# Cross-attention's inputs loaded and prepared during self-attention, and a round's turns ahead of the pair's output projection

## What is computed

```python
x = x + attn(layernorm(x), wq, wk, wv, wo)                 # 16 heads of 64
x = x + xattn(layernorm(x), ctx, mask, Wq, bq, Wk, bk, Wv, bv, Wo, bo)   # 16 heads of 16
x = x + ffn(layernorm(x), ...)                             # 8 experts, one per token
```

## Time and profile before

| | |
|---|---|
| median of 3 runs | 1658.84 us (1657.04 to 1662.4) |
| profiled execution, in all | 1658.88 us |
| its span | 1657.1 us |
| busy in the span: TensorE | 1446.5 us (87%) |
| VectorE | 962.8 us (58%) |
| ScalarE | 760.2 us (46%) |
| Pool | 563.7 us (34%) |

### The profile page before, as it was taken

How to read it: one execution, slowest core, us unless ns; L and a number is a source line. 1 busy time by engine, 2 the same in 40 slices (tenths; PEclk the granted TensorE clock), 3 DMA queues, 4 the chain that set the end, 5 groups by cost and what they waited for, 6 DMA issues and landing times. The chain is left out here.

```text
span 1657.1 us, 39281 instructions
## 1 busy us (share of the span) xinstructions
PE 1446.5 (87%) x12244; PEld 1250.0 (75%) x12244; DVE 962.8 (58%) x2371; ACT 760.2 (46%) x1830; POOL 563.7 (34%) x692
## 2 busy tenths in 40 slices
PE   4789899999999998479999999999986119999997
PEld 3688878888887877368888888888866118888886
DVE  5547475656566665157777777767653215555553
ACT  4547464655555565035655555555651002222221
POOL 5244353525252617512222222222202443333332
PEclk9899999999999999679999999999995559999999
DMA  5703030303021221387676666767621413555551
GB/s 180 208 2 81 1 79 2 77 13 66 17 62 34 45 44 37 78 216 193 179 198 180 189 186 184 199 176 200 172 73 53 143 57 126 188 184 189 180 182 51
DMA packets 159950, 195.71 MB, mean 118 GB/s; under 512 B 83724, under 2 KB 128307, under 8 KB 159636
## 3 DMA queue, kind: packets, MB, share of 16 engines
q1 hardware_dynamic: 154356, 186.09, 40.6%
q0 software_dynamic: 3968, 6.59, 1.2%
q10 hardware_dynamic: 1568, 2.30, 0.5%
HBM read 138.63 MB, written 58.05 MB: 119 GB/s over the span
## 5 line engine op out<-in xcount | busy, mean ns | idle before, releaser
L1209 DVE TENSOR_REDUCE row_max<-psb_s 100x1 f32<-100x361 f32 x512 | 263.4, 531 | 140.1 <-PE psb_s L1352 134.2
L1101 ACT ACTIVATE probs<-psb_t 121x400 f32<-121x400 f32 (+1 forms) x384 | 190.5, 508 | 115.2 <-PE psb_t L1362 112.5
L1352 PE MATMUL psb_s<-k,q 97*100 97x362 f32 x512 | 185.3, 364 | 15.2 <-DVE row_max L1209 9.4
L437 POOL TENSOR_TENSOR diag<-neg_ident,row_max 100x400 fp32r<-100x400 f32 x128 | 112.2, 898 | 183.0 <-DVE row_max L529 158.2
L1362 PE MATMUL psb_t<-q,k 98*121 98x200 f32 (+1 forms) x768 | 147.5, 274 | 1.9 <-ACT probs L1101 1.7
L2032 PE MATMUL psd_h<-h_in,w_sb 128*128 128x256 f32 x640 | 144.2, 384 | 1.4 <-ACT h_in L1898 1.4
L2040 PE MATMUL psd_y<-w_sb,hid 128*128 128x256 f32 x640 | 144.5, 379 | 0.0
L2032 PEld LDWEIGHTS psd_h<-h_in,w_sb 128*128 128x128 f32 x640 | 123.5, 193 | 19.0 <-issue 1.8
L2040 PEld LDWEIGHTS psd_y<-w_sb,hid 128*128 128x128 f32 x640 | 120.1, 190 | 15.5
L1362 PEld LDWEIGHTS psb_t<-q,k 98*121 98x121 f32 (+1 forms) x768 | 125.4, 184 | 6.1 <-ACT probs L1101 2.7
L1352 PEld LDWEIGHTS psb_s<-k,q 97*100 97x100 f32 x512 | 85.7, 168 | 41.5 <-DVE row_max L1209 27.2
(11 more groups left out here) (226 smaller groups left out, 3604.6 us busy)
## 6 DMA issues: line engine op xcount, KB each, us to landing
w_sb<-in_w SPq DMA_DIRECT2D x40, 1024.0 KB, 7.6
packed_keys<-k_st SPq DMA_DIRECT2D x32, 724.0 KB, 3.5
k<-packed_keys SPq DMA_DIRECT2D x64, 362.0 KB
v_rows<-v_tok SPq DMA_DIRECT2D x32, 400.0 KB
v_ext<-v_rows SPq DMA_DIRECT2D x32, 400.0 KB
q<-packed_queries SPq DMA_DIRECT2D x64, 200.0 KB
k<-packed_keys SPq DMA_DIRECT2D x64, 181.0 KB
c_t<-in_contextT SPq DMA_DIRECT2D x32, 361.0 KB, 4.6
```

What stands on the lines that cost most here:

```text
L437: pool.tensor_tensor(diag[:, g % 2], c.neg_ident[0:S, 0:S].unsqueeze(1).to_broadcast([S, GH, S]), row_max[:, g // 2 % 2, g % 2].unsqueeze( ...
L1101: act.activation(probs[0:KT[kt], u % 2, kt], ps_t[i % 2][0:KT[kt], 0:4 * S], ACT.Exp, scale=HD2 ** -0.5).then_inc(probs_ready, 1)
L1209: dve.reduce_max(row_max[:, p, h:h + 1], ps_s[h % 2][0:S, 0:S2], AX_X).then_inc(max_ready, 1)
L1352: pe.matmul(ps_s[h % 2][0:S, 0:S2E], q2[0:97, p, u, g, S * a:S * (a + 1)], k2[0:97, p, u, g], start=True, stop=True).then_inc(scores_ready, 1)
```

## The change

Two edits, and what they need.

1. Cross-attention's buffers for wk, wv, wq, the biases, the masks and the first context now lie in `c.stage`, the same memory as w_stage, which outlives self-attention. o_part moves to its end. SP takes quad 0 out of its loop and issues the loads of `cross_inputs` behind quad 0's value transfers. Pool clears the mask buffers behind the weight split and computes the masks ahead of the last quad. wo and bo are loaded at the start of cross-attention behind the second context. Rows q2[96] and k2[97] get their ones by two loads from HBM instead of two memsets on Pool. At the start of cross-attention Pool begins with split_context(0), and all engines put the first keys ahead of the first turned x. normalize(0) on VectorE stands behind keys(0, 0, 0). The clearing of v_ext comes behind split_context(1).
2. In self-attention TensorE's turns of round r-2 stand ahead of the pair's projection.

Some semaphores that nobody waits for are shared between blocks.

```diff
 def self_attention (SP):
+            def cross_inputs():
+                sp.wait_ge(vo_lo_ready, 2)
+                for dst, src in ((c.wk_st, cross["wk"]), (c.wv_st, cross["wv"]), (c.wq_sb, cross["wq"])):
+                    sp.dma_start(dst, src.rearrange("(k p) n -> p k n", p=128)).then_inc(c.cross["w2_loaded"], 16)
+                for dst, src in ((c.bq_sb, cross["bq"]), (c.bk_sb, cross["bk"]), (c.bv_sb, cross["bv"])):
+                    sp.dma_start(dst, src).then_inc(c.cross["w2_loaded"], 16)
+                sp.dma_start(c.first_context, cross["ctxT"][0].rearrange("(k p) s -> p k s", p=128)
+                             ).then_inc(c.cross["ctx_loaded"], 16)
+                sp.dma_start(cross["qd"]..., c.empty...).then_inc(c.cross["q_cleared"], 16)
+                sp.dma_start(cross["ones"], c.ones_f[:]).then_inc(c.cross["ones_stored"], 16)
+                sp.wait_ge(c.cross["mask_cleared"], 2)
+                for kt in range(3):
+                    sp.dma_start(c.mask_t[0:KT[kt], kt, :], cross["maskT"][KT0[kt]:KT0[kt] + KT[kt], :]
+                                 ).then_inc(c.cross["mask_t_loaded"], 16)
+                sp.dma_start(c.mask_b[:, 0:S2], cross["mask"]).then_inc(c.cross["mask_b_loaded"], 16)
+            values_through(0)
+            cross_inputs()
+            with sp.Fori(1, QUADS) as q:
+                values_through(q)
+            sp.wait_ge(c.cross["bias_ready"], 1)
+            sp.dma_start(cross["kb"], c.bias_b.bitcast(F32)).then_inc(c.cross["bias_stored"], 16)
+            sp.wait_ge(c.cross["bias_stored"], 16)
+            sp.wait_ge(c.cross["ones_stored"], 16)
+            sp.wait_ge(c.cross["q_cleared"], 16)
 (Pool):
             split_weights(1)
+            pool.wait_ge(vo_lo_ready, 2)
+            pool.memset(c.mask_t, 0).then_inc(c.cross["mask_cleared"], 1)
+            pool.memset(c.mask_b, 1).then_inc(c.cross["mask_cleared"], 1)
...
             with pool.Fori(1, QUADS - 1) as q:
                 quad(q, False)
+            cross_masks()
             quad(QUADS - 1, True)
 (TensorE), in iteration r, behind the diagonals:
+                    for g in in_round(r - 2):
+                        ...  (the turns of L702)
                     for g in in_round(r - 3):
                         if last_round_of_pair(r - 3):
                             ...  (the projection)
-                    for g in in_round(r - 2):
-                        ...  (the turns of L702)
 def cross_attention (SP):
             context(1, 1)
+            sp.dma_start(wo_sb, wo.rearrange("(k p) n -> p k n", p=128)).then_inc(wo_loaded, 16)
+            sp.dma_start(bo_sb, bo...to_broadcast([S, D])).then_inc(wo_loaded, 16)
+            sp.dma_start(q2[96:97]..., ones(16 * 2 * S)).then_inc(ones_placed, 16)
+            sp.dma_start(k2[97:98]..., ones(16 * S2E)).then_inc(ones_placed, 16)
 (Pool):
+            split_context(0, 0)
             inverse_root(0)
-            split_context(0, 0)
+            split_context(1, 1)
             inverse_root(1)
-            split_context(1, 1)
+            pool.memset(v_ext[:, :, :, :, HD2:32], 0.0).then_inc(pad_ready, 1)
 (VectorE):
-            dve.wait_ge(w_lo_ready, 2)
             norm_stats(0)
+            low_bits(0, wk_hi, wk_lo, wk_st)
+            low_bits(1, wv_hi, wv_lo, wv_st)
+            keys(0, 0, 0)
             normalize(0)
             norm_stats(1)
             normalize(1)
             norm_stats(2)
-            keys(0, 0, 0)
 (TensorE):
-            pe.wait_ge(w_loaded, 16 * 8)
-            pe.wait_ge(w_hi_ready, 2)
-            pe.wait_ge(w_lo_ready, 2)
-            pe.wait_ge(pad_ready, 5)
+            pe.wait_ge(w_loaded, 16 * 6)
+            pe.wait_ge(w_lo_ready, 1)
+            pe.wait_ge(pad_ready, 2)
+            keys(-2, 0, 0)
             turn_x(-3, 1)
-            keys(-2, 0, 0)
...
+            pe.wait_ge(w_lo_ready, 2)
             values(-1, 1, 0)
+            pe.wait_ge(ones_placed, 32)
```

More of the change, by code:

```diff
@@ L109, in at_batch, with stage_for_cross_attention, take, weight @@
     return tensor[:, bass.ds(b, 1), cols].rearrange("p b d -> p (b d)")
-def self_attention(nc, c, x, wqkT, wvT, woT, v_dram, xs):
+def stage_for_cross_attention(c, ctx, nc):
+    at = [0]
+    def take(words):
+        at[0] += words
+        return c.stage[:, at[0] - words:at[0]]
+    def weight():
+        return take(KD * D).rearrange("p (k n) -> p k n", k=KD)
+    c.wk_st, c.wv_st, c.wq_sb = weight(), weight(), weight()
+    c.bq_sb, c.bk_sb, c.bv_sb = take(KD), take(KD), take(KD)
+    c.mask_t, c.key_dead, c.key_live = (take(3 * B)[0:KT[0]].rearrange("p (k b) -> p k b", k=3) for _ in range(3))
+    c.mask_t = c.mask_t.bitcast(I32)
+    c.mask_b = take(S2E)[0:B].bitcast(I32)
+    c.bias_b = take(S2E)[0:B].bitcast(F32R)
+    c.first_context = take(KD * S2).rearrange("p (k s) -> p k s", k=KD)
+    at[0] = 2 * KD * O1 - 4 * (S // GB) * NT
+    c.wo_sb = weight()
+    c.bo_sb = take(D)[0:S]
+    for name in ("w2_loaded", "mask_cleared", "mask_t_loaded", "mask_b_loaded", "key_mask_ready", "bias_ready",
+                 "bias_stored", "ctx_loaded", "q_cleared", "ones_stored"):
+        c.cross[name] = ctx.enter_context(nc.semaphore(name + "_x"))
+def self_attention(nc, c, x, wqkT, wvT, woT, v_dram, xs, cross):
     with ExitStack() as ctx:
@@ L679, in quad @@
                                   skip_group_check=True).then_inc(shifted_ready, 1)
+                    for g in in_round(r - 2):
+                        pe.wait_ge(o_ready, q * GQ + (g + 1))
+                        if g == 0:
+                            reach(pe, x1_ready, q * QUAD)
+                        if g >= 2:
+                            pe.wait_ge(ot_copied_act, q * 2 * GQ + 2 * (g - g % 2))
+                        for w in range(2):
+                            ins = pe.transpose(ps_ot[:, 2 * S * (g % 2) + S * w:2 * S * (g % 2) + S * (w + 1)],
+                                               o_norm[:, g % 2, 128 * w:128 * (w + 1)], c.ident[0:S, 0:S])
+                        ins.then_inc(ot_ready, 1)
                     for g in in_round(r - 3):
@@ L969, in step @@
                     place(b + 2, p)
-            sp.wait_ge(q_cleared, 16)
             place(0, 0)
```

169 lines of the change are left out of this document (73 added, 96 removed).

## The result

The changed kernel takes 1637.33 us (median of four executions, 1635.16 to 1639.22); the kernel before, executed beside it, 1657.94 (1653.13 to 1662.4). The ratio is 0.9872, with an interval of 0.9844 to 0.9900: 20.6 us faster, where 16.7 were worked out. The profiled spans are 1634.5 and 1657.1 us, 22.6 us apart.

What follows compares the result with a forecast made beforehand. TensorE was taken to bound what follows its hollow at the change to cross-attention. An earlier start (14.4 us) and the turns (2.3) sum to 16.7 us, giving a 1640.4 us span and 1642.1 us time, range 1636 to 1649.

Steps and rivals of the forecast that it cites:

- The bound: TensorE's hollow at the change to cross-attention, a 21.3 us wait for xn; earlier first scores should carry to the end.
- Cost 0 for what moved: Loads, small memsets and mask operations moved into self-attention fit in idle time; SP's 10.2 us of issuing fits into 55.7.
- Step 1 and 2: From T, SP's first issue of cross-attention: Pool's split to T+2.7, plus 0.69 us for VectorE's wk subtraction, first keys T+3.4.
- The barrier: Start of cross-attention: TensorE and ScalarE starting behind the barrier cost 0, with up to 3 us left in the range.
- Step 3 and 4: First keys' matmuls and low part free VectorE at T+6.8; normalize(0), beside Pool's second context, ends at T+7.9.
- Step 5: Turn of xn, its copy and the first queries in cross-attention: queries' low part ready at T+12.3.
- Step 6: Stores and packed loads before the first scores, untouched: 11.5 us, first scores at T+23.8 against T+38.2, gain 14.4 us.
- The turns, 8 x 0.29: Self-attention, round 6 of each quad: turns inside TensorE's 1.68 us wait for o_lo gain 2.3 us, bounds 0 and 4.1.
- The kinder clock: Rival at cross-attention's start: clock stays 2.4 GHz or engines do not hold; gain 18 to 22, about 1638.5 us, chance 0.2.
- A new wait: Rival: late engines, Pool's second context ahead of normalize(0), or packed loads meeting other transfers; 1648 us, chance 0.2.
- The slower rival: Self-attention: turns ahead of the projection wait for a late o_norm; at 3.9 us late about 1662 us, chance 0.03.
- The change doesn't do what it says: Rival: first scores wait for something that stays, so cross-attention's start moves by less than 4 us; 1655 us, chance 0.04.

Runs made afterwards that it cites:

- the loads alone: The changed kernel with the pair's projection put back ahead of TensorE's turns in self-attention; 1644.84 us, ratio 0.9899.
- the clearing late: The changed kernel with SP's clearing of routed_rows issued behind the moved cross-attention loads instead of ahead of quad 0's value stores; 1630.25 us, ratio 0.9818.
- wv later: The changed kernel with VectorE's wv subtraction behind keys(0,0,0), normalize(0) and norm_stats(1); 1640.84 us in one execution.
- the turns alone: The kernel before with only TensorE's turns of round r-2 moved ahead of the pair's projection; 1654.78 us, ratio 0.9972.

## Why the prediction was right, point by point

- **The bound.** Right. The hollow was the place, and the shift of the first scores was kept: 532.36 and 532.19 us from there to routing.
- **Cost 0 for what moved.** Right. SP's moved loads stand after quad 0's value loads, in order of time in the changed kernel:

```profile
71.33 2.22 SPq L338 DMA_DIRECT2D v_ext<-v_rows  x2
73.59 2.57 SPq L345 DMA_DIRECT2D stage<-in_wk2T  x1
...
84.53 0.32 SPq L357 DMA_DIRECT2D stage<-in_mask  x1
```

  They end at 84.85 us, 11.3 us of issuing where 10.2 were put, long ahead of the store of quad 1. The sum left out the store of ones, 3.28 us, and read the end of the old list at 683.66, where the load of the mask behind it ends at 684.03. No wait of TensorE or VectorE is new there.
- **Step 1 and 2, first keys at T+3.4.** T+3.08. c_lo took 1.91 us beside the subtraction of wk against 1.58 alone: the two do hold each other off, but Pool lost 0.33 and not the whole 0.69, since wk's subtraction had begun 0.31 us ahead of c_lo. The Trainium skill says that Pool contends with VectorE instructions that have two SBUF inputs (GPSIMD Engine Reference, 1. Specifications). The trace agrees: both subtractions have two, and they grew from 1.58 to 1.91 (c_lo) and from 0.66 to 2.07 us (wv_lo).
- **The barrier.** Up to 3 us were left in the range for a late start of ScalarE and TensorE. ScalarE starts at T+0.02, and TensorE 0.14 us behind the end of c_lo: nothing.
- **Step 3 and 4, xn at T+7.9.** It ended at 673.37, T+6.8, below the lower bound of 7.2. VectorE was free at T+6.2 instead of T+6.8, half of that from step 2. The second context had landed within 4.2 us and Pool began it at T+4.2, so that when xn started at 672.79 only the last 0.43 us of Pool's subtraction (671.64 to 673.22) were left: xn took 0.58 us, not some 1.1.
- **Step 5, T+12.3.** T+11.37, early by 0.93 because of step 4 (from xn to the low part 4.57 us passed, 4.4 were put).
- **Step 6, 11.5 us to the first scores.** 12.46 in this trace, and 11.32 in the changed kernel's second. SP's issues of the keys' store and of the first packed keys, in order of time, before and then after (first trace):

```profile
702.78 0.60 SPq L929 DMA_DIRECT2D packed_keys<-k_st  x1
...
706.35 1.11 SPq L955 DMA_DIRECT2D k<-packed_keys  x2
```

```profile
680.52 0.60 SPq L978 DMA_DIRECT2D packed_keys<-k_st  x1
...
685.39 1.11 SPq L1004 DMA_DIRECT2D k<-packed_keys  x2
```

  Both kernels issue the keys' store 2.5 us behind the queries' first, but from it to the load of what it stored pass 3.57 us before and 4.87 after; the rest is 0.3 shorter. This 0.95 cancels the 0.93 of step 5, so that T+23.8 comes out to the tenth by luck: with the fast landing the first scores stand at T+22.7, 1.1 us ahead of the forecast.

  The sum had no term for a landing that varies. It is 3.4 to 3.7 us in eight of the twelve traces, and 4.9 to 5.3 in four: the changed kernel's first, the loads alone, the clearing late and wv later. Those four have one thing in common. While the keys' store is under way, a transfer of instructions (queue q8, 16 KB) runs on the core's DMA engines too. In the changed kernel's first trace, 680.52 to 685.39 us (number, MB, share of 16 engines; then KB and us to landing):

```profile
q8 instruction: 1, 0.02, 2.0%
...
packed_keys<-k_st SPq DMA_DIRECT2D x1, 724.0 KB, 4.9
```

  It began 0.4 to 1.1 us behind the issue of the store in the four and lasted 1.3 to 1.7 us, about what the store is late by; in the eight others no transfer of instructions falls between the issue of the store and its landing. In the first trace the queries' stores were late too: SP's packed loads of the queries start 3.1 us behind the end of their last issue, against 1.5 before. No run moves that transfer, so the cause is argued from twelve traces and not shown by an experiment.
- **The turns, 8 x 0.29.** 8 x 0.36. The mechanism is as told: the turns went inside the wait, and the projection itself starts 2.3 us behind the diagonals in both. Next scores start 5.76 us behind the projection's first matmul instead of 6.06 (244.66 to 250.42, 248.06 to 254.12), which is the 0.29 of the sum. The other 0.06 was not foreseen: without the turns right ahead of them, the four next scores take 0.46 us up to the following products, where they took 0.52 (250.42 to 250.88, 254.12 to 254.64).
- **Sum.** 14.3 + 2.8 = 17.1 us against 16.7. The measured 20.6 has an interval of 16.6 to 25.9 and holds both. The further 5.5 us between the spans are no gain of the change as far as the traces show: the prologue (2.7, of which 2.0 are a wait that varies from one execution to the next in either kernel), less time at the lower clock (1.4), and 1.4 behind the first scores, which is within what the traces differ by (routing and experts took 411.8 to 413.5 us over all kernels here).
- **The kinder clock.** Fell: the clock fell at about T+3.3, when TensorE had stood idle for its 4.16 us and the first keys had just begun, and keys, turn and queries ran at 0.50, the level of 1.2 GHz. Kinder holding was part of it (step 2), and worth 0.3 us.
- **A new wait.** None of the three named came: the engines started at once, Pool's second context cost xn less than was put, and TensorE's list has no wait for the ones. What came in their place in the first trace is the slower keys' store, at 1.3 us.
- **The slower rival.** Fell: one wait of 0.3 us for o_norm, as before, and the turns alone make the kernel faster.
- **The change doesn't do what it says.** Fell, but it shows where it would have been true: loads or ones alone, left at the start, cost 7 to 8 us.

## What to carry to other kernels

At a change of stage, find every chain that leads to the first matmul (loads, Pool's clearing, the masks) and move them all: here either of two, left behind, kept 7 to 8 of some 14 us. Where the total of a sum comes out right, check its steps all the same; two were off by 1 us here in opposite directions, and a second trace of the same kernel showed it. A bulk transfer on a queue belongs behind the first small stores that an engine waits for.

## What was not expected of the hardware

- A clearing of 5140 KB ahead of two stores of 400 KB on the same queue stretched their issuing from 3.05 to 11.79 us. TensorE waited 5.9 to 9.1 us for it, the longer the closer the stores came behind the clearing.
- The first store of 724 KB in cross-attention landed in 3.4 to 3.7 us, or in 4.9 to 5.3 where a transfer of 16 KB of instructions fell into it, and in either time in the two traces of one kernel (4.9, 3.5).
- Where Pool and VectorE held each other off, the instruction that began second paid: Pool's subtraction grew by 0.33 us (1.58 to 1.91) behind wk's, VectorE's by 1.4 (0.66 to 2.07) behind Pool's.
